# Layer 2's attention by diagonal blocks and states, and a scan whose growth streams its columns twice

## The reference

```python
q, k = jax.nn.silu(q), jax.nn.silu(k)
q, k = _lrpe(q, theta, n), _lrpe(k, theta, n)      # concat(x * cos(th), x * sin(th))
mask = jnp.exp(slope_rate * tril)
energy = jnp.einsum('bhne,bhme->bhnm', q, k) * mask[None]
out = jnp.einsum('bhnm,bhmd->bhnd', energy, v)
out = u * _srmsnorm(out)                           # joined heads, x * rsqrt(mean(x*x) + eps)
out = out @ out_w.T + out_b
```

## Time and profile before

| | |
|---|---|
| median of 3 executions | 3019.97 us (3019.44 to 3028.2) |
| the profiled execution's own time | 3005.36 us |
| its span | 3003.4 us |
| granted clock over the span | 0.761 |
| busy over the span | PE 2038.8, DVE 1895.8, ACT 1162.0, POOL 745.3 us |
| layer-1 scan | 684.7 to 781.3 us |
| layer-2 attention behind its first norm | 1368.5 to 1575.8 us |

### The profile page before, as it was taken

The page is one execution under the profiler, slowest core; times in us unless marked ns, Lnnn a source line. Parts: engine busy times, 40 slices in busy tenths (PEclk is TensorE's granted clock), DMA queues, the critical chain, the costliest instruction groups (busy, mean ns, idle before and its releaser), DMA issues. The chain is left out here.

```text
span 3003.4 us, 36146 instructions
## 1 busy us (share of the span) xinstructions
PE 2038.8 (68%) x10967; PEld 1190.2 (40%) x10978; DVE 1895.8 (63%) x5609; ACT 1162.0 (39%) x3146; POOL 745.3 (25%) x612
## 2 busy tenths in 40 slices
PE   6977769438779998796974835565655555565256
PEld 2643446235446665443642513333333333242042
DVE  4234322476656555572344578999999999446945
ACT  3643322313146666114003623555555555422111
POOL 1100143043333332001100301333333333204400
PEclk7988889755789999897886866666575656667568
DMA  4000011300000000001000000000000000000000
GB/s 164 2 1 0 23 39 35 116 1 2 2 1 1 1 1 1 0 0 80 0 0 0 1 0 1 1 1 1 1 1 1 1 1 1 1 0 0 0 1 14
DMA packets 9639, 37.11 MB, mean 12 GB/s; under 512 B 1707, under 2 KB 6960, under 8 KB 8192
## 3 DMA queue, kind: packets, MB, share of 16 engines
q1 hardware_dynamic: 7424, 31.75, 2.7%
q0 software_dynamic: 2048, 3.38, 0.5%
HBM read 30.18 MB, written 5.77 MB: 12 GB/s over the span
## 5 line engine op out<-in xcount | busy, mean ns | idle before, releaser
L3221 PE MATMUL psum<-work 32*128 32x256 f32 x512 | 131.6, 659 | 297.8 <-ACT work L3316 297.8
L3368 DVE MATCH_REPLACE8 work<-work 128x256 f32<-128x256 f32 x768 | 306.9, 416 | 0.0
L3416 POOL TENSOR_TENSOR work<-work 128x1024 f32<-128x1024 f32 x64 | 150.7, 2355 | 513.2 <-ACT work L3316 513.2
L3365 DVE MAX8 work<-work 128x8 f32<-128x256 f32 x768 | 268.1, 416 | 0.0
L3221 PEld LDWEIGHTS psum<-work 32*128 32x128 f32 x512 | 78.4, 314 | 325.1 <-ACT work L3316 167.8
L483 POOL TENSOR_TENSOR work<-work 128x256 f32<-128x256 f32 (+2 forms) x144 | 133.5, 946 | 265.6 <-DVE work L743 265.6
L673 ACT ACTIVATE work<-work 128x128 f32<-128x128 f32 (+1 forms) x320 | 144.9, 454 | 41.2 <-PE psum L543 24.6
L235 DVE RECIPROCAL work<-work 128x256 f32<-128x256 f32 x40 | 70.0, 1750 | 123.0 <-ACT work L268 123.0
L3316 ACT ACTIVATE work<-work 128x256 f32<-128x256 f32 x256 | 128.1, 501 | 0.0
L3244 PE MATMUL psum<-work,tiles 128*8 128x256 f32 x512 | 116.5, 607 | 13.6 <-ACT work L3325 13.6
L3418 POOL TENSOR_TENSOR work<-work 128x1024 f32<-128x1024 f32 x64 | 121.2, 1894 | 6.2 <-DVE work L3390 1.2
(11 more groups left out here) (564 smaller groups left out, 5064.7 us busy)
## 6 DMA issues: line engine op xcount, KB each, us to landing
big_weights<-L0f_dram SPq DMA_DIRECT2D x1, 6053.5 KB, 26.0
big_weights<-L_dram SPq DMA_DIRECT2D x1, 5858.0 KB, 17.4
big_weights<-L_dram SPq DMA_DIRECT2D x1, 4952.5 KB, 16.2
big_weights<-L_dram SPq DMA_DIRECT2D x1, 2187.0 KB, 20.5
big_weights<-L_dram SPq DMA_DIRECT2D x1, 1630.5 KB, 12.0
big_weights<-L0f_dram SPq DMA_DIRECT2D x1, 1630.5 KB, 6.8
slots_in<-tiles SPq DMA_DIRECT2D x1, 1280.0 KB, 9.3
residual<-x_dram SPq DMA_DIRECT2D x1, 1024.0 KB, 4.9
```

Of the source, the lines that this page charges most:

```text
L3221: mm = nc.tensor.matmul(scores(n)[:, u, :], qb[head, tile % 2, u % 2 * P:(u % 2 + 1) * P], kb[head, tile % 2, :], start=True, stop=True, t ...
L3365: ch.step(v.max(top8[:, n % 2, u, r, :], src[:, u, :]))
L3368: ins = v.match_replace(raw[:, n % 2, u, :], top8[:, n % 2, u, r, :], src[:, u, :], REPLACED)
L3416: ch.link(g.tensor_tensor(mine, mine, rest[:, n % 2], ALU.subtract))
```

## The change

Layer 2's attention loop makes scores in the two diagonal 128x128 blocks of a head alone, four heads side by side in the four bands, and the two blocks off the diagonal go by a state: the keys of the other tile, turned by four transposes, times the values of that tile, scaled by `factor` (exp(slope) or 1, and 0 outside a head's own block), times the queries. `rotary_projection` holds the tables and the projections in one stage: the 20 matmuls start at its start, ScalarE makes the sines ahead of the first read, and VectorE makes the mask tables from 8 exponentials. The values are read from `c.HN` without a copy, and q and k rotate through three buffers instead of two. The norm behind it takes `times=u`: VectorE multiplies with `u` at its start, ahead of the scaling. The loop is written out in full instead of `Fori`.

In layer 1, `grow` streams the same 128 columns of `U` twice, into 256 columns of the bank, of which `keep` reads the first 128; `rest` moves to the third 128 columns. `delta_layouts` ends with two more matmuls of 512 columns, whose result isn't read.

```diff
...
+            for i in range(0 if times is None else NC):
+                nc.vector.tensor_tensor(dst[:, ch[i]], src[:, ch[i]], times[:, ch[i]], ALU.mult).then_inc(c.weighted.sem, 1)
...
+            kept(pe, 7)
+            for n in range(2):
+                nc.tensor.matmul(c.psum[:, 7, :], ident, c.CT[:, n * CH:(n + 1) * CH], start=True, stop=True)
...
-                    mm = nc.tensor.matmul(grown(z)[:, tau ^ r, :], kt[band[r], t, 4 * z + (tau ^ r), :],
-                                          U[band[r], group(z, k), :], start=True, stop=True, tile_position=(32 * r, 0))
+                    out = c.psum[:, 4 * z + (tau ^ r), 0:2 * P].rearrange("p (n x) -> p n x", x=P)
+                    twice = U[band[r], group(z, k), :].unsqueeze(1).broadcast_to([32, 2, P])
+                    mm = nc.tensor.matmul(out, kt[band[r], t, 4 * z + (tau ^ r), :], twice, start=True, stop=True,
+                                          tile_position=(32 * r, 0))
...
+            for n, (i, j) in enumerate(steps):
+                src, w = jobs[j][0:2]
+                if n >= 8:
+                    pe.wait_ge(c.product_taken.sem, c.product_taken.at(n - 7))
+                nc.tensor.matmul(c.psum[:, n % 8, :], w, src[:, i * CH:(i + 1) * CH], start=True, stop=True) \
...
+            nc.scalar.activation(grow, c.w("L2a_slope"), ACT.Exp).then_inc(c.rates_ready.sem, 1)
+            act.wait_ge(c.angles_ready.sem, c.angles_ready.at(1))
+            ch.link(nc.scalar.activation(absr, r, ACT.Abs))
+            nc.scalar.activation(sn, r, ACT.Sin)
+            nc.scalar.activation(cs, absr, ACT.Sin, scale=-1.0, bias=c.w("half_pi")).then_inc(c.tables_ready.sem, 1)
+            for n, (i, j) in enumerate(steps):
+                _, _, bias, func, out = jobs[j]
+                act.wait_ge(c.product_ready.sem, c.product_ready.at(n + 1))
+                nc.scalar.activation(out[:, i * CH:(i + 1) * CH], c.psum[:, n % 8, :], func, bias=bias) \
...
+            for h in range(H):
+                ch.step(v.scalar_tensor_tensor(decay[:, h, :], lower, grow[:, h:h + 1], c.w("L2a_upper"), ALU.mult, ALU.add))
...
+            def score(b, t):
+                n = 2 * b + t
+                pe.wait_ge(c.rotated.sem, c.rotated.at(b + 1))
+                if n:
+                    pe.wait_ge(c.scores_masked.sem, c.scores_masked.at(n))
+                for kt in range(2):
+                    for r in range(4):
+                        band = slice(32 * r, 32 * r + 32)
+                        mm = nc.tensor.matmul(scores[:, r, kt, :], keys(b)[band, t, half[kt]], queries(b)[band, t, half[kt]],
+                                              start=True, stop=True, tile_position=(32 * r, 0))
+                mm.then_inc(c.scores_ready.sem, 1)
+
...
+            def make_states(b):
+                pe.wait_ge(c.v_taken.sem, c.v_taken.at(b + 1))
+                pe.wait_ge(c.keys_kept.sem, c.keys_kept.at(b + 1))
+                for t in range(2):
+                    for kt in range(2):
+                        mm = nc.tensor.matmul(made_states[:, t, kt, :], ktok[:, b % 2, t, kt, :], value_places(b, kt, t),
+                                              start=True, stop=True)
+                mm.then_inc(c.states_made.sem, 1)
+
+            def mix(b):
+                pe.wait_ge(c.scores_masked.sem, c.scores_masked.at(2 * b + 2))
+                pe.wait_ge(c.states_scaled.sem, c.states_scaled.at(b + 1))
+                if b >= 2:
+                    pe.wait_ge(c.out_copied.sem, c.out_copied.at(b - 1))
+                for qt in range(2):
+                    for t in range(2):
+                        nc.tensor.matmul(out(b)[64 * t:64 * t + 64, half[qt]], states[:, b % 2, t, 1 - qt, :],
+                                         queries(b)[:, t, half[qt]], start=True, stop=False, tile_position=(0, 64 * t))
+                    for e in range(2):
+                        for p in range(4):
+                            band, lo = slice(32 * p, 32 * p + 32), (2 * p + e) * 32
+                            mm = nc.tensor.matmul(out(b)[band, half[qt]], vpad[:, b % 2, qt, lo:lo + 32],
+                                                  en[b % 2][p // 2][:, p % 2 * 2 + e, qt, :], start=False, stop=(e == 1),
+                                                  tile_position=(0, 32 * p))
+                mm.then_inc(c.mixed_ready.sem, 1)
+
+            turn(0)
+            make_values(0)
+            for b in range(B):
+                score(b, 0)
+                make_states(b)
+                if b:
+                    mix(b - 1)
+                score(b, 1)
+                if b + 1 < B:
+                    turn(b + 1)
+                    make_values(b + 1)
+            mix(B - 1)
+
...
+            keep_keys(0)
+            for b in range(B):
+                if b + 1 < B:
+                    keep_keys(b + 1)
+                act.wait_ge(c.mixed_ready.sem, c.mixed_ready.at(b + 1))
+                nc.scalar.copy(q0[:, b * S:(b + 1) * S], out(b)).then_inc(c.out_copied.sem, 1)
...
+                v.tensor_tensor(en[b % 2][t], scores, decay[:, 4 * t:4 * t + 4, :].unsqueeze(2)
+                                .broadcast_to([P, 4, 2, P]), ALU.mult).then_inc(c.scores_masked.sem, 1)
...
+            dve.wait_ge(c.zeros_made.sem, c.zeros_made.at(1))
+            take_values(0)
+            for b in range(B):
+                mask(b, 0)
+                scale(b)
+                mask(b, 1)
+                if b + 1 < B:
+                    take_values(b + 1)
...
-    with nc.Block() as block:
-        @block.vector
-        def _(dve):
-            nc.vector.tensor_copy(c.T[:, 1, :], u)
...
-    with nc.Block() as block:
-        @block.vector
-        def _(dve):
-            nc.vector.tensor_tensor(c.T[:, 0, :], c.T[:, 0, :], c.T[:, 1, :], ALU.mult)
...
+                    g.memset(vpad, 0.0).then_inc(c.zeros_made.sem, 1)
+                if b >= 3:
+                    pool.wait_ge(c.mixed_ready.sem, c.mixed_ready.at(b - 2))
+                seq = slice(b * S, (b + 1) * S)
+                for t, (q, k) in enumerate(((q0, k0), (q1, k1))):
+                    g.tensor_tensor(queries(b)[:, t, :], q[:, seq], trig[:, t, :], ALU.mult)
+                    ins = g.tensor_tensor(keys(b)[:, t, :], k[:, seq], trig[:, t, :], ALU.mult)
+                ins.then_inc(c.rotated.sem, 1)
...
+    gated = c.T[:, 1, :]
+    norm_stage(c, q0, gated, "eps6", centre=False, times=u)
+    project_stage(c, [([gated], [c.w("L2a_wo")], c.w("L2a_bo"), None, c.X, c.X)])
```

244 lines of the change are left out of this document (122 added, 122 removed).

## The result

The changed kernel takes 2896.86 us (median of 4 runs, 2892.37 to 2899.49) where the kernel before took 3019.7 beside it: ratio 0.9592, 95% interval 0.9562 to 0.9623. The forecast was 2892, with a range of 2868 to 2920. The profiled execution took 2898.0 us, its span 2896.2.

A forecast was written before the change was run, and what follows sets the result against it. It took TensorE's own length to bound the attention loop and a serial chain at 1.2 GHz the scan. 6.4 + 104.7 + 3.8 + 12.9 = 127.8 us off 3005.4 gave 2877.6; plus 14.6 to the median, 2892, range 2868 to 2920.

The forecast's parts named there:

- The scan: Layer 1's scan: 256-column growths keep the clock warm, saving 11.5 us; 12.9 us with the neighbouring stages.
- The chain of a step: In the scan, growth, keep, prediction and update in series: 2.75 us before, 2.42 warm with 256-column growths, 3.18 cold.
- Rival 1: The scan stays cold despite 256 columns: about +18 us instead of -12.9, kernel at 2923 us; chance 0.15.
- Its milder half: In the scan, the clock falls at the start alone and rises again; cost between warm and cold scan, no own chance.
- The argument from the outputs: Outputs hold clock 1.00 with 256-column products though TensorE idles more than in the scan; so 256-column growths should warm the scan.
- Its fillers: Two matmuls ahead of the barrier before the scan: cost +1.1 us, and shorten TensorE's idle time there.
- The outputs: Stage behind the scan: its first two placings and first scores would be warm too, saving 2.3 us.
- The attention loop: Layer 2's loop: 48.8 us against 153.5, gain 104.7 us; bounds 34 and 70 us.
- the chain for a sequence: In the attention loop: values 0.5, states 1.0, mixing of the sequence before 1.4, second scores 0.74, mask 1.22: 4.9 us.
- strips in turn: Upper bound in the attention loop: 64-column strips run one after another, state weights not hidden, +1.4 us a sequence.
- Tables and projections: Stage ahead of the attention loop: projections start while angles are made, 20 reads take 14.0 us; gain 6.4 us.
- Behind the loop: After the attention loop: the copy stage goes (1.4 us) and the product with u goes (2.4 us); gain 3.8 us.

## Why the prediction was right, by its steps

- **The scan: right, in kind and size.** It named the clock, not fewer instructions, as what the change buys; undoing the columns alone gives 12 us back at 0.50. The forecast was 11.5, measured is 11.9. The chain of a step was worked out as 2.75 us before and 2.42 after; plain steps took 2.82 and 2.50, which is the forecast difference. (The 12.9 us with the neighbours hold 0.2 "of rounding in the waits" that no row shows.) Rival 1, in which the scan stays cold, did not come, and its price holds: doubled growths at the low clock cost 0.67 us a step more, 20.8 over the scan, where some 20 were put down. Its milder half, a fall at the start and a rise, did come in six later kernels. Records cover 84.46 of 96.3 us in the cold scan and 67.55 of 84.8 in the warm one, so idle time does not tell them apart. That was the rule of the Trainium skill (TensorE: Matmul & The Clock Gate, section HAM oscillation) behind rival 1, and no run here bears it out for this stage.
- **Its reason for the clock: not settled.** The argument from the outputs was loose, for two of their products (L2472 and L2486) have 128 columns as well, and the share of time in which columns go in rises by half at one and the same clock only. And the filler beside the growths streams about as many columns as the doubling, but left the clock low for 68 us. That doubled growths bring the clock back and single ones don't is shown; why is not.
- **Its fillers: wrong.** They were to shorten TensorE's idle time ahead of the scan. Without them the scan was the same, and with them the clock still fell about 3 us into the scan in all six kernels with growths doubled, in one or both halves, whose layouts ended at 686 to 688 us; they cost 1.0 us. That the changed kernel's scan was warm throughout was not their doing, and the prediction has no term that decides it: the scan is 85.0 us where the clock did not fall, 87.0 to 90.5 where it did and rose again 7 to 24 us later. So the 11.9 us are in part luck; where the clock fell, the gain was 6.4 to 9.9.
- **The outputs: luck.** Forecast -2.3, measured -2.5. But with the same code and the same doubled growths ahead five kernels took 58.5 to 58.6 us for them, more than the 56.4 of before. Scan and outputs together took 139 to 149 us with both halves' growths doubled, in eight kernels, and 153 to 157 with single ones, in three: the difference is 4 us at the least and 18 at the most.
- **The attention loop: right in kind, 4.3 us short (53.1 for 48.8).** The failed step is "the chain for a sequence". It had the values' 0.5 where the first score's 0.65 stands, no hand-overs, and the mixing at 12 passes of 0.12 = 1.4 where 1.88 is measured. What is missing there is a term for the change of the weights' shape: four of them, each about 0.1 us longer than a pass. The bound "strips in turn" (+1.4) covered the amount, not the reason: strips of 64 columns do run side by side. That could have been read in the kernel before, of which the prediction says that no trace has such strips: in layer 1's cross-attention (L603, at 941.39 us) pairs of them start 0.007 us apart, and passes 0.11 apart. Pitch 5.74 instead of 4.9, six times: +5.0. The first sequence and the end behind the last first mask are 0.6 longer each. The cold start cost 2.0 in this profile, the difference to the kernel with loop fillers (1.8 in the first sequence, 0.2 in the second), where 4 were taken. The time to the first mask was 4.7, forecast 4.8.
- **Tables and projections: 2.2 better than forecast,** 21.2 us where 23.4 were worked out. The sum put 20 reads of 0.69 to 0.70 us end to end; they took 0.69 to 0.80 each, but started 0.57 apart, overlapping. Behind the loop: -4.4 for -3.8.
- **The sum: near, with luck.** The profiled execution missed 2877.6 by 20.4 us: +18.7 in stages ahead of the changed ones (16.1 of it in layer 0's experts), +1.2 in the changed ones, +5.2 between them, -4.7 behind. Nothing in the prediction foresaw the 18.7. It added 14.6 us, the distance of the earlier execution from the median, without a cause; that this was the same difference in the experts is likely, but no profile of the slower executions shows it. So the changed stages were forecast within 1.2 us, by misses that cancel (the loop's gain came out 4.0 short, that of the tables 2.2 larger), and the whole within 5 us by a difference in code that is the same.

## What to carry to other kernels

A product repeated into columns that nobody reads can pay where a serial chain of small matmuls runs at 1.2 GHz; weigh it by running it with one more copy (here 7.6 us), and find which of the products stand on the chain at all: taking half of the doubling away gave nothing back. Count the changes of the weights' shape in a row of small products, not only the products: here each stood for 0.20 us from start to start, where a pass stood for 0.09 to 0.11. For a pipelined loop write down the chain from a buffer's release to its next release, with each piece of work that stands ahead of the release on the in-order engine; a piece cut in two there gained 0.33 us a sequence at no cost. Before comparing two profiles, take out the stages whose code is the same.

## What was not expected of the hardware

- The same scan code took 85.0 us where the clock, risen among the layouts' matmuls at 695.6 to 698.4, kept up, and 87.0 to 90.5 where it had risen at 679.3 to 681.4, fell 3 us into the scan, and rose again 7 to 20 us later. Why it falls once in one case and not in the other, at the same instructions, is open. The first case is that of the profiles with the experts at 224.5 us, the second that of 208.3, so the chip and the moment of the scan's start are rivals that no run here parts.
- Growths of 128 columns with nothing beside them: clock 0.50 from about the fourth microsecond to the end, in all three kernels, of both groups; of 256: 1.00 once risen, to the scan's end, in all eight.
- The outputs behind the scan took 54.0 us (two kernels) or 58.5 to 58.6 (five) with the same code and the same doubled growths ahead, as the clock kept up or was low twice in their first 20 us, for 3.4 and 10.2 us.
- A change of the weights' shape costs TensorE the same whichever the shapes: 0.20 us from start to start, 128*64 to 128*32 as well as 32*128 to 128*128.
